# A two-layer attention and mixture-of-experts kernel: layer 0 experts from contiguous groups, the second norm and routing inside layer 1's attention

## The reference, cut to what matters

```python
xn = layernorm(x)
x = x + L0_attn(xn) + L0_ffn(xn)      # linear attention, 16 heads, 2 kernels; top-1 MoE
xn = layernorm(x)
x = x + L1_attn(xn) + L1_ffn(xn)      # window and latent attention; top-2 MoE

# L0_attn: q, ks, vs from xn (with biases); per batch and head
state = prod_over_kernels(ks^T vs);  out = layernorm(q @ state) @ Wo.T + bo
# L0_ffn
probs = softmax(xn @ router_w.T + router_b);  top1 = argmax(probs)
y = (xn @ expert_w[top1].T + expert_b[top1]) * max(probs)         # 8 experts, 128 x 128
# L1_attn: softmax over a window of 32 to 64 keys, plus softmax over 64 pooled latents, gated
# L1_ffn: two of 8 experts per token: relu(xn @ w1 + b1) @ w2 + b2, F = 512
```

## Time and profile before

| what | us |
|---|---|
| median of 3 runs (740.57 to 745.67) | 741.97 |
| the profiled execution | 738.12 |
| its span (mean granted PE clock 0.834) | 736.4 |
| PE busy / weight loads / DVE / ACT / POOL | 523.8 / 423.5 / 400.4 / 291.6 / 254.3 |
| start of the first layer 1 query matmul (L1357) | 263.99 |
| end of layer 1's attention, about | 531 |

### The profile page before, as it was taken

The page is one execution under the profiler, slowest core; times in us unless marked ns, Lnnn a source line. Parts: engine busy times, 40 slices in busy tenths (PEclk is TensorE's granted clock), DMA queues, the critical chain, the costliest instruction groups (busy, mean ns, idle before and its releaser), DMA issues.

```text
span 736.4 us, 20789 instructions
## 1 busy us (share of the span) xinstructions
PE 523.8 (71%) x7157; PEld 423.5 (58%) x7161; DVE 400.4 (54%) x1082; ACT 291.6 (40%) x746; POOL 254.3 (35%) x303
## 2 busy tenths in 40 slices
PE   2939628876305658788887888777689999999940
PEld 1917527665304634556566465654478888888840
DVE  6498726776069477785957768688301111111117
ACT  1307602444101232543435344353146555555524
POOL 6066653665580004533426130000014343434430
PEclk9659857999655557997989789999679999999985
DMA  9996124333124000100001000000044444444539
GB/s 236 232 238 113 43 65 130 112 111 114 55 70 159 1 1 28 44 23 24 29 21 42 17 29 3 3 4 2 15 148 165 158 162 156 167 153 166 173 101 283
DMA packets 80938, 69.83 MB, mean 95 GB/s; under 512 B 8452, under 2 KB 66499, under 8 KB 80862
## 3 DMA queue, kind: packets, MB, share of 16 engines
q1 hardware_dynamic: 71696, 55.00, 26.8%
q0 software_dynamic: 6624, 12.70, 5.3%
q10 hardware_dynamic: 2542, 1.08, 0.6%
HBM read 22.66 MB, written 23.22 MB: 62 GB/s over the span
## 4 chain that ended last, share of the span: by engine, by line
PE 30%; SPq 16%; DVE 16%; issue 14%; DMA 8%; POOL 7%; ACT 6%; ACTq 1%; POOLq 0%; DVEq 0%
SPq L1102 6%; SPq L1115 5%; SPq L1125 4%; DMA ydram<-arena,g_id 4%; PE psum L1374 3%; POOL ydram L824 3%; PE psum L551 3%; ACT arena L1503 2%; PE psum L1429 2%; PE psum L1389 2%; PE psum L1357 2%; POOL sorted L683 2%; DVE arena L1619 2%; DVE arena L1622 2%; DMA arena<-ydram 2%
## 5 line engine op out<-in xcount | busy, mean ns | idle before, releaser
L683 POOL DMA_INDIRECT sorted<-xr_all,slot x96 | 95.9, 999 | 170.7 <-DVE arena L1622 132.5
L1214 POOL DMA_INDIRECT ydram<-arena,f_id x71 | 69.7, 982 | 206.6 <-DVE f_id L1190 194.0
L1175 ACT ACTIVATE arena<-psum,b1T 128x128 f32<-128x128 f32 x284 | 81.3, 369 | 78.5 <-PE psum L1144 74.1
L1198 DVE TENSOR_TENSOR arena<-psum,b_bc 128x128 f32<-128x128 f32 x71 | 20.7, 292 | 145.2 <-PE psum L1155 142.6
L1144 PE MATMUL psum<-arena 128*128 128x128 f32 x568 | 82.7, 290 | 13.7 <-DMA arena<-arena 10.5
L1144 PEld LDWEIGHTS psum<-arena 128*128 128x128 f32 x568 | 71.3, 197 | 26.7 <-issue 17.2
L1155 PE MATMUL psum<-w,arena 128*128 x568 | 81.7, 287 | 0.5 <-issue 0.4
L1155 PEld LDWEIGHTS psum<-w,arena 128*128 128x128 f32 x568 | 69.7, 193 | 4.5 <-issue 1.2
L824 POOL DMA_INDIRECT ydram<-arena,g_id x40 | 43.3, 1083 | 47.4 <-DVE arena L813 21.3
L1539 ACT ACTIVATE arena<-arena 128x512 f32<-128x512 f32 x32 | 20.2, 632 | 68.3 <-DVE arena L1622 68.2
L1397 PE MATMUL psum<-arena 128*128 128x128 f32 (+3 forms) x64 | 25.9, 517 | 18.7 <-DVE arena L1659 13.3
(11 more groups left out here) (282 smaller groups left out, 1130.8 us busy)
## 6 DMA issues: line engine op xcount, KB each, us to landing
arena<-arena SPq DMA_DIRECT2D x71, 256.0 KB, 2.4
arena<-ydram SPq DMA_DIRECT2D x24, 256.0 KB, 4.4
arena<-mix SPq DMA_DIRECT2D x40, 128.0 KB
sorted<-pre_row SPq DMA_DIRECT2D x1, 4680.0 KB, 29.9
arena<-sorted SPq DMA_DIRECT2D x71, 65.0 KB, 1.8
sorted<-pre_row SPq DMA_DIRECT2D x1, 2600.0 KB, 21.5
arena<-sorted SPq DMA_DIRECT2D x10, 260.0 KB, 2.9
x_all<-in_L_attn_x_dram SPq DMA_DIRECT2D x8, 256.0 KB, 6.8
```

What stands on the lines that cost most here:

```text
L683: g.indirect_dma_start(out=dst, out_offset=bass.IndirectOffsetOnAxis(ap=slot[:, choice, t:t + 1], axis=0), in_=xr_all[:, t, :], in_offset= ...
L1175: ins = act.activation(f_hT[rr % 4][:, j * P:(j + 1) * P], psum[:, 2 + rr % 2, j * P:(j + 1) * P], ACT.Relu, bias=b1T[:, bass.ds(e * FC + ...
L1214: g.indirect_dma_start(out=ydram, out_offset=bass.IndirectOffsetOnAxis(ap=f_id[rr][:, :], axis=0), in_=f_y[rr], in_offset=None, bounds_che ...
```

## The change

1. `setup_pe` begins with 28 bf16 matmuls of 512 columns on a constant (their results are not used), then waits for the weights as before.
2. The biases come in as 88 partitions of 16 values, are split by POOL there, and SP moves the parts by DMA into rows of `b3`, which now also holds the experts' biases (`expert_b`). PE adds a group's bias with a matmul on a part of `b3` that is chosen at run time.
3. Routing 0's small matmuls move inside the first feature stage (the order is then `wait, features(0), routing0_pe`), and the expert numbers get their own signal (`s_exp`), after the one for slots.
4. The 32 scatters of layer 0 are released three per feature stage; a row has 128 values and no longer the token's number.
5. Layer 0's experts: `TURNS` and `WORKS` say which groups are transposed and multiplied in a stage: two groups in each of stages 3 to 7, none in the others. PE reads the expert numbers itself (L851, a value load for each tile) and takes weights and biases in place; ACT copies results and transposes; SP stores the result as it lies (no scatter). When all ten groups are stored, POOL gathers them back by slot, one indirect DMA for each tile (32), into four buffers. The sum into x moves from POOL to DVE (L1092).
6. Norm 1: the first pair of batches is normalised before attention, the statistics of pairs 1, 2 and 3 stand inside the attention of batch 0 (both halves) and batch 1; rows are made by ACT (L630), transposes and logits of PE go through the ring. Routing 1 stands in pieces inside batches 1 and 2. Its 64 scatters are paced from the end of batch 2 to batch 7. Two barriers of three go.
7. In the attention, projections GX and GQ move ahead of `values(b, 1)`, `latent_operands` ahead of `normalise(b, 1)`; w1 comes in eight pieces.

```diff
         def setup_pe(pe):
+            pe.wait_ge(s_pool, 2)
+            for _ in range(28):
+                pe.matmul(psum[:, 0, :], onesb[:, 0:P], onesb[:, :], start=True, stop=True)
             pe.wait_ge(s_const, 2)
...
+        def group_pe(pe, k):
+            if k:
+                pe.wait_ge(g_yr, k)
+            else:
+                pe.wait_ge(s_exp, 1)
+            pe.wait_ge(g_xTr, k + 1)
+            chosen = []
             for j in range(4):
+                e = pe.value_load(expert[0:1, 0, 4 * k + j:4 * k + j + 1], min_val=0, max_val=E - 1)
+                pe.matmul(psum[:, 3, j * C:(j + 1) * C], onesb[:, 0:P], b3[:, bass.ds(e * C + 3 * C, C)],
+                          start=(j == 0), stop=False, skip_group_check=True)
+                chosen.append(e)
+            for j, e in enumerate(chosen):
+                mm = pe.matmul(psum[:, 3, j * C:(j + 1) * C], g_xT[k % 2][:, j * P:(j + 1) * P],
+                               weT[:, bass.ds(e, 1), :].rearrange("p a c -> p (a c)"), start=False, stop=True,
+                               skip_group_check=True)
...
-        def state_act(act, three, two, one, grp):
+        def state_act(act, three, two, one, turn, work):
...
+            for k in work[:1]:
+                group_act(act, k)
+            for k in turn[:1]:
+                group_turn_act(act, k)
             if three:
...
+        TURNS = [(), (), (0,), (1, 2), (3, 4), (5, 6), (7, 8), (9,), (), ()]
+        WORKS = [(), (), (), (0, 1), (2, 3), (4, 5), (6, 7), (8, 9), (), ()]
...
         def attn1_dve(v, ch):
...
+                if b == 0:
+                    norm1_statistics(v, ch, 1)
+                if b == 1:
+                    norm1_statistics(v, ch, 3)
+                if b == 2:
+                    route_gates(v, ch, 1)
                 window_softmax(2 * b + 1)
...
+                if b == 0:
+                    norm1_statistics(v, ch, 2)
+                    v.wait_ge(c_init, 2)
+                if b == 1:
+                    for i in range(NP2):
+                        emptied(v, "lg", i)
+                    route_first(v, ch)
                 window_softmax(2 * b + 2)
+                latent_operands(b + 1)
...
         def _(v):
...
-            phase_end(v, 1)
-            v.wait_ge(s_sc, 16 * NT)
-            v.wait_ge(b_xu, 1 + B)
-            norm_dve(v, 1)
-            phase_end(v, 2)
-            routing_dve(v, 1)
-            v.wait_ge(c_init, 1)
-            attn1_dve(v)
+            phase_done(v)
+            ch = Chain(v, s_chain)
+            norm1_statistics(v, ch, 0)
+            norm1_inverses(v, ch, 0)
+            v.wait_ge(s_phase, 3)
+            attn1_dve(v, ch)
```

More of the change, by code:

```diff
@@ new lines, in norm1_statistics @@
+        def norm1_statistics(v, ch, i):
+            for b in (2 * i, 2 * i + 1):
+                v.wait_ge(s_yl[b % 4], 64 * (i // 2 + 1))
+                for t in range(T):
+                    n = b * T + t
+                    ch.after(v.scalar_tensor_tensor(out=flat(x_all, n), in0=yl[b % 4][:, t, :],
+                                                    scalar=gate[:, 0, n:n + 1], in1=flat(x_all, n),
+                                                    op0=ALU.mult, op1=ALU.add))
+            ch.sync()
+            v.sem_inc(s_yu, 2)
+            for n in range(i * 2 * T, (i + 1) * 2 * T):
+                ch.after(v.bn_stats(flat(st_all, n), flat(x_all, n)))
+            ch.sync()
+            variances(v, ch, i)
@@ new lines, in norm1_inverses, with norm1_rows @@
+        def norm1_inverses(v, ch, i):
+            v.wait_ge(s_root, NP2 + i + 1)
+            inverses(v, ch, i)
+            v.engine_nop().then_inc(s_rn, 1)
+        def norm1_rows(act, i):
+            act.wait_ge(s_rn, i + 1)
+            for b in (2 * i, 2 * i + 1):
+                for t in range(T):
+                    n = b * T + t
+                    ins = act.activation(xr_all[:, n, 0:C], flat(x_all, n), ACT.Identity, bias=mean[:, n:n + 1],
+                                         scale=rstd[:, n:n + 1])
+                ins.then_inc(s_xn, 1)
@@ L829, in feat_pe, with group_act @@
+        def group_act(act, k):
+            act.wait_ge(g_yp, k + 1)
+            if k >= 2:
+                act.wait_ge(g_st[k % 2], 16 * (k // 2))
+            act.activation(g_y[k % 2].rearrange("p j c -> p (j c)"), psum[:, 3, :], ACT.Copy).then_inc(g_yr, 1)
         def feat_pe(pe, prev, cur):
@@ L905, in roots_dve, with state_pe @@
             v.sem_inc(b_all, 1)
-        def state_pe(pe, three, two, one, grp):
+        def state_pe(pe, three, two, one, turn, work):
             if two:
@@ L974, in state_act @@
                 act.activation(a_oT, psum[:, 6, :], ACT.Copy).then_inc(b_oTs, 1)
-                group_act(act, grp)
-            if three:
-                b = batch(three)
-                act.wait_ge(b_wo, b + 1)
-                act.wait_ge(b_xu, b + 1)
-                act.activation(a_w, psum[:, 7, :], ACT.Copy).then_inc(b_w, 1)
+            for k in work[1:]:
+                group_act(act, k)
+            for k in turn[1:]:
+                group_turn_act(act, k)
             if one:
@@ L989, in state_act, with state_dve @@
                 act.activation(a_ve[:, :], a_ve[:, :], ACT.Sqrt).then_inc(b_sq, 1)
-            if not three:
-                group_act(act, grp)
-        def state_dve(v, three, two, one, grp):
+        def state_dve(v, three, two, one):
             ch = Chain(v, s_chain)
@@ L1460, in remote @@
                 mm.then_inc(rdy, 1)
-            for name in first:
+            rows_turned(0)
+            rows_turned(1)
+            for name in ("Q", "K", "V", "GX", "GQ", "G"):
                 project(name, 0)
+            logits(0)
             scores(0)
@@ L1793, in _ @@
             biases_pool(g)
-            scatter_pool(g, 0, 0, sorted0)
-            states(g, state_pool)
-            group_pool(g, (B + 1, 0))
-            attn1_init(g)
+            scatter_pool(g, 0, 0, s0_rows)
+            for r in range(2):
+                g.wait_ge(g_st[r], 16 * (NGR // 2))
+            gather_pool(g, 0)
+            attn1_init(g, 0)
+            gather_pool(g, 1)
+            attn1_init(g, 1)
+            gather_pool(g, 2)
+            gather_pool(g, 3)
             scatter_pool(g, 1, 0, sorted1)
```

725 lines of the change are left out of this document (398 added, 327 removed).

## The result

The changed kernel takes 754.46 us (median of 4 runs, 751.33 to 755.46); the kernel before, run beside it, 741.27 us (738.78 to 745.67). The ratio is 1.016 with a 95% interval of 1.011 to 1.022: slower by some 13 us. Each ratio in this text that has an interval is formed from the undisturbed runs of both kernels, and can differ from the ratio of the medians. The profiled execution took 755.46 us, its span is 753.7.

What follows compares the result with a forecast made beforehand. It took POOL's queue, a 9 us wait and a 57 us serial stretch as what bounds. 738.1 - 14.6 + 30.5 - 47.4 + 36 = 742.6, with 3.9 for the median 746.5 us; range 712 to 776.

Steps and rivals of the forecast that it cites:

- A: From the start up to the stages with groups: warm-up, biases and the wait for the first group, together -14.6 us.
- B: Layer 0's states from stage 3: two groups a stage with value loads on PE, 19 us a stage, +30.5 us.
- C: Norm 1 and routing 1 between the layers: 57.6 us shrink to one pair's 10.2, so -47.4 us.
- D: Layer 1 attention takes in three pairs' statistics, routing 1, rows and table loads: +36 us, bounds 10 and 47.5.
- The marks that the prediction set itself: Prediction wrong if first query matmul starts before 215 or after 250, or attention's first three batches take under 100 or over 140 us.
- the -3.7 for routing 0: Start: bias work on POOL no longer slows DVE's routing 0 operations (1.25 against 0.42 us); -3.7, bounds -1 and -5.
- the lower bound of 11.3: Group stages 3 to 7: shortest stage foreseen, 11.3 us, with value loads hidden behind matmuls already queued.
- R1: Group stages: value loads hide and the clock stays up, a stage takes 13 us, total 716.5; chance 0.21.
- R3: Group stages: PE falls to 1.2 GHz and stays, a stage takes 23 us, total 766.5; chance 0.28.
- the one on what fills DVE's idle times: Layer 1 attention: 32 us of added DVE work against 26 us idle; in fixed order mostly serial, hence +36.
- R2: Layer 1 attention: moved pieces fill DVE's idle times, adding 14 us instead of 36, total 724.5; chance 0.14.
- The two rules: Skill's figures, not used: 600 ns floor per value load (median 758); 1.38 us drain per table load (about 755).

Runs made afterwards that it cites:

- four-edit kernel: Changed kernel with value loads early, norm 1's PE work later, no warm-up, and ACT's normalised output ahead of the first group's copies: ratio 0.967, 757.4 us on another chip.
- three-edit one: Changed kernel with value loads early, norm 1's PE work later and no warm-up: 727.4 us, ratio 0.981 to the kernel before.

## Why the prediction was right, and where it was off

The forecast was a small loss or none by two large terms that nearly cancel, 746.5 us in a range of 712 to 776, with slower (0.41) the likeliest of the three outcomes. Measured is 754.5, slower by 1.6%. The nearness of the two numbers is in part luck. The profiled execution was forecast at 742.6 and took 755.5, 13 more: A came out 5.8 above its term, B 6.3 below, C 1.5 above and D 11.5 above. And the median of the kernel before lay 3.9 above its profiled execution, that of the changed one 1.0 below. The marks that the prediction set itself were kept, one of them barely: first query matmul at 233.4 (215 to 250), the attention's first three batches 136.8 us (100 to 140).

**A, start.** Predicted -14.6, measured -8.8. The 9.23 us of waiting for the first group went, as said. What did not arrive is the -3.7 for routing 0. The chain itself did get shorter, by 4.0 us without the wait named below: its operations come at 0.42 us and not at up to 1.25. But it began 2.5 us later (39.46 in place of 36.94 us), because in this execution norm 0 ran at the lower clock throughout, where before it had a stretch at the upper one (16 to 24 us, granted 1.00 against 0.50); and DVE then waited 2.09 us for the two routing matmuls behind the first features:

```profile
46.19 0.42 DVE L677 COPY ra<-psum 128x256 f32<-128x256 f32 x1 [2.09 <-PE psum L742]
```

The first varies from run to run: the first T(G) stood between 95.8 and 101.5 us in nine profiled runs that share this start, with the warm-up or without it (101.3 here). The second was a cost of a moved step that the sum had left out; the run with these matmuls first gave about 3 us back at the first T(G).

**B, the states.** The stage was 17.1 us (18.5 for the first) where 19 was taken, and what follows the last of these stages 15.3 where 13 was taken. The step was right: POOL's queue went, PE's value loads took its place, and the clock ran at both levels (0.78 from 120 to 206 us against 1.00 in the earlier trace rows). Its sizes were not all right: eight loads cost 3.4 us and not 5.6, the clock's part included, while the step that put one ACT copy of 0.6 us ahead of the normalised output was too low. There are two copies, and the first waits for the first group's products; with the old order back the stage lost another 2.3 us, the clock's part included (0.88 to 1.00), though on another chip. With both mended it is 11.8 us at the upper clock, close to the lower bound of 11.3. The 2 us that the sum had for the lower clock have no run of their own: the mean granted clock rose in each run that took idle time out (0.80, 0.88, 1.00). (The 1.1 us for the second group's products is right as the busy time of the earlier trace rows; 8 times 277 ns would be 2.2, but these matmuls overlap.) R1's mechanism, loads hidden behind queued matmuls, is real for the second group. For the first it isn't, since nothing is queued there; the run with early loads made it so for both. R3 did not come: PE was back at the upper level in every stage.

**C, norm 1 and routing 1 outside.** 11.7 us for 10.2. Right, within 1.5 us.

**D, the attention.** Predicted +36 with 47.5 as the upper bound, measured +47.5 between the first and last keys, although the last three batches came out 7.5 us shorter, of which the sum had 2 at most. The term that was mis-sized is D, and the step in it is the one on what fills DVE's idle times: it charged DVE's and ACT's added work, and gave no price to PE's place in the order. The prediction had seen that order (it stands against R2 as a reason) but its sum has no us for it. Norm 1's transposes and logits were put ahead of scores that need nothing of them, and PE, in order, made DVE wait 10.5, 9.5 and 10.5 us. Moving that part, with one piece of routing 1, gave 16 us back. The reordered projections were taken for 2 us and are worth 16 to 18 alone and 7 here. Between the two, the mistakes partly cancelled. R2, that attention absorbs the pieces, did not come: in the change's order the three pairs cost 45 us inside, as against 49 outside, where POOL's gathers set the pace. With PE's part later they cost about 30.

**The two rules.** `tensor_load` took 298 ns on PE (median of 40), and with early loads the 40 cost 0.3 to 0.4 us a stage: the floor of about 600 ns in the Trainium skill ("DMA: Bandwidth & Descriptors", "Latency and other measured facts") doesn't hold here. Taking the six table loads away changed the time by 0.5 us, so the drain that the Trainium skill ("ScalarE: Activation LUTs", "What ACT_TABLE_LOAD costs") adds to each is either absent or hidden with it; the run doesn't tell these apart.

What stays open: how much of D belongs to routing 1. With norm 1 outside, batches 2 and 3 were 36.4 and 39.6 us against 30.3 and 29.2 with the new order alone, which suggests 17 us, about DVE's 15.4 in the earlier trace rows. No run took routing 1 alone out.

## What to carry to other kernels

Moving a serial stretch into a pipelined one hides it only if every engine meets it at a place where its next pipelined step does not stand behind it: before adding up busy times, read for each engine which instruction stands right behind the inserted wait, and who waits for that one. A value load cost next to nothing here behind queued matmuls or ahead of a wait, and held the next matmul back to 0.8 us behind the one before where it stood between short ones. Savings that were measured one by one need not add: 18 and 16 us gave 27. And test the smallest part of a large change alone: here the reorder of a few lines was worth more than all the rest, which without it is a loss.

## What the runs showed of the hardware

- A value load on PE's queue is 298 ns, with a register operation of 151 ns behind it; bias matmuls with one between them are 0.78 to 0.86 us apart, and without it about 0.1 (0.39 us for four).
- PE's clock went down and up again in each of the five group stages, so that eight matmuls took 1.91 us (L978, at 164.8 us) and eight like them 1.05 us (L993, at 169.3 us), at a steady pitch of 17.0 to 17.1 us from the second on. With the same matmuls closer together the mean granted clock was 0.88 (stages of 13.7 and 14.0 us) and 1.00 (11.8 us) in place of 0.80.
- The kernel before took 735 to 742 us (medians) in four sessions and 784.9 us in a fifth, on another chip, with 780 to 792 in all its 11 runs. The four-edit kernel's attention (first to last keys) took 278.5 us there, against 252.8 for the three-edit one elsewhere, and from the last keys to the end 264.7 against 253.1, while in a window of the experts (560 to 700 us) PE was busy alike (128.5 and 130.0 us). The kernel before has no trace from that chip, so how much of this is the chip's and how much the fourth edit's is open.
